# Masks of two batch pairs in one matmul, and instruction lists ordered by a new table, in a five-layer attention kernel

## The reference, cut to what matters

```python
def attention(q_src, kv_src, Wq, Wk, Wv, mask):      # in every layer
    scores = einsum("bhqd,bhkd->bhqk", heads(q_src @ Wq), heads(kv_src @ Wk)) / sqrt(8)
    return einsum("bhqk,bhkd->bhqd", softmax(where(mask, scores, -inf)), heads(kv_src @ Wv))

x = ln(x + attention(x, x, ...) @ Wo)                 # sa: no mask
x = ln(x + attention(x, ctx, ...) @ Wo)               # ca: head h sees keys k with (k - h) % 4 == 0
x = ln(x + gelu(x @ W1) @ W2)                         # f
x = ln(x + concat(x, attention(x, ctx, ...) @ Wout) @ Wupd)   # l1: one key mask per batch
x = ln(x + attention(x, ctx, ...))                    # l2: causal mask
x = x + gelu(x @ W1) @ W2                             # g
w = square(relu(scores(rmsnorm(x), rmsnorm(ctx))))    # l3: where |key - idx[token]| <= 1
x = x + (w / max(sum(w), 1e-6)) @ v @ Wo
```

## Time and profile before

| | |
|---|---|
| median of 3 runs | 227.08 us (224.49 to 230.85) |
| profiled execution | 224.79 us, span of its instructions 222.2 us |
| TensorE busy | 193.2 us, 4951 matmuls and as many weight loads |
| VectorE, ScalarE, GpSimd busy | 128.7, 119.9, 36.0 us |
| mean granted TensorE clock | 0.977 of full |

### The profile page before, as it was taken

One profiled execution on the slowest core, in us unless ns is written; L12 is line 12 of the kernel. 1 busy time (PEld: TensorE's weight loads), 2 busy tenths in 40 slices (PEclk: granted clock), 3 DMA queues, 4 the chain that ended last, 5 costly groups with the idle time before them and its releaser, 6 DMA issues.

```text
span 222.2 us, 11019 instructions
## 1 busy us (share of the span) xinstructions
PE 193.2 (87%) x4951; PEld 147.3 (66%) x4951; DVE 128.7 (58%) x227; ACT 119.9 (54%) x308; POOL 36.0 (16%) x61
## 2 busy tenths in 40 slices
PE   2798789999999999989798878899997799899935
PEld 0376568767886787668565656667686648588834
DVE  0599999996745227942378744442835226555950
ACT  1254740674756777477625652744769436763802
POOL 2990300131120131112011000111010003100000
PEclk9999996999999999999999999999999769999999
DMA  5990000000000000000000000000000000000002
GB/s 140 372 379 20 0 6 4 6 4 3 6 3 3 0 3 0 3 3 3 4 6 3 3 6 3 3 6 3 3 3 3 6 3 1 3 3 3 6 27 71
DMA packets 3901, 6.25 MB, mean 28 GB/s; under 512 B 528, under 2 KB 3216, under 8 KB 3600
## 3 DMA queue, kind: packets, MB, share of 16 engines
q1 hardware_dynamic: 3856, 5.57, 7.4%
HBM read 5.04 MB, written 0.52 MB: 25 GB/s over the span
## 4 chain that ended last, share of the span: by engine, by line
PE 67%; issue 9%; ACT 6%; DVE 5%; POOLq 1%; POOL 1%; DVEq 0%; ACTq 0%
PE bank L453 31%; PE score L456 20%; PE bank L697 12%; PE bank L669 4%; ACT probs_sb L801 2%; DVE probs_sb L1042 2%; ACT att_sb L845 1%; DVE m_col_sb L963 1%; POOLq L323 1%; DVE v_ext_sb L936 1%; DVE att_sb L1027 1%; ACT L801 1%; DVE v_ext_sb L933 1%; ACT xa_sb L850 0%; ACT probs_sb L799 0%
## 5 line engine op out<-in xcount | busy, mean ns | idle before, releaser
L963 DVE TENSOR_REDUCE m_col_sb<-score 128x32 f32<-128x2048 f32 (+1 forms) x16 | 30.2, 1889 | 11.8 <-PE score L456 11.6
L453 PE MATMUL bank<-v_ext_sb,probs_sb 128*32 128x18 f32 (+1 forms) x2176 | 28.5, 193 | 8.1 <-issue 6.4
L453 PEld LDWEIGHTS bank<-v_ext_sb,probs_sb 128*32 128x32 f32 x2176 | 24.7, 115 | 15.3 <-issue 13.5
L801 ACT ACTIVATE probs_sb<-score 128x1024 f32<-128x1024 f32 (+1 forms) x28 | 26.2, 962 | 13.0 <-PE score L456 12.9
L1082 POOL TENSOR_SCALAR vare_sb<-var_sb 128x2 f32<-128x2 f32 x20 | 5.2, 261 | 140.7 <-ACT att_sb L845 140.7
L453 PE MATMUL bank<-xa_sb,W_sb 128*128 128x256 f32 x64 | 21.3, 448 | 6.9 <-DMA W_sb<-in_mats 3.3
L905 DVE TENSOR_TENSOR k_heads_sb<-k_kept_sb,small_sb 128x1024 f32<-128x1024 f32 x12 | 14.7, 1226 | 16.5 <-ACT k_kept_sb L820 16.4
L914 DVE TENSOR_TENSOR q_heads_sb<-q_kept_sb,small_sb 128x1024 f32<-128x1024 f32 x16 | 19.5, 1222 | 6.5 <-ACT q_kept_sb L810 3.8
L845 ACT ACTIVATE att_sb<-bank 128x128 f32<-128x128 f32 x40 | 10.7, 274 | 21.5 <-PE bank L697 21.4
L456 PE MATMUL score<-k_heads_sb,q_kept_sb 32*64 32x256 f32 x384 | 18.0, 413 | 3.0 <-issue 2.2
L456 PE MATMUL score<-q_heads_sb,k_kept_sb 32*64 32x256 f32 x512 | 20.1, 400 | 0.4 <-issue 0.4
(11 more groups left out here) (120 smaller groups left out, 360.6 us busy)
## 6 DMA issues: line engine op xcount, KB each, us to landing
W_sb<-in_mats SPq DMA_DIRECT2D x1, 1152.0 KB, 7.6
W_sb<-in_mats SPq DMA_DIRECT2D x1, 1024.0 KB, 9.8
ctxT_sb<-in_ctxT SPq DMA_DIRECT2D x1, 512.0 KB, 5.1
cn_sb<-in_ctx SPq DMA_DIRECT2D x1, 512.0 KB, 11.3
hid_sb<-in_idx SPq DMA_DIRECT2D x1, 512.0 KB, 7.3
out<-attT_sb SPq DMA_DIRECT2D x4, 128.0 KB, 1.8
xa_sb<-in_xT SPq DMA_DIRECT2D x1, 384.0 KB, 3.9
W_sb<-in_mats SPq DMA_DIRECT2D x1, 192.0 KB, 2.8
```

The costliest lines, as they stand in the source:

```text
L453: return pe.matmul(o, l, r, start=start, stop=stop)
L801: act.activation(dst, src, ACT.Exp, scale=SCALE).then_inc(sem("exp"), 1)
L963: dve.tensor_reduce(o, src, AX.X, ALU.max).then_inc(sem("max"), 1)
```

## The change

1. Masks. In `scores` the loop over masks stands before the loop over j and a mask matmul writes both pairs at once: 512 columns, one x, one r. In `scores_t` the same for l2 and l3; l1's stays one j at a time, since its stationary operand is the key mask of the batch.
2. The planner. `records(k)` gives the number of instructions of each TensorE job, `fetched(...)` lets the program arrive in blocks of 256 of them, FETCH = 3.7 us apart, and delays a job by what has not arrived. Costs of pieces are replaced, SLOW is gone, HOP is 0.23 for 0.2, LEAD 8.3 for 5.3, and `AHEAD` is a new table, with entries for single groups as well ("flip_x ca 3").
3. Thereby the order of the lists of all engines.

```diff
+def records(k):
+
+    step, name, g, i = k
+    masks = {"s l1": 16, "s l2": 32, "t l1": 32, "t l2": 32, "t l3": 32}.get(f"{step} {name}", 0)
+    return masks + {"k": 5, "q": 5, "v": 9, "ctx_rows": 5, "m": 5, "flip": 5, "flip_x": 5, "h": 9, "y": 17, "ms": 9,
+                    "out": 17, "z": 44 if name == "f" else 20, "av": 66 if name == "ca" else 130, "s": 66,
+                    "t": {"ca": 83, "l3": 66}.get(name, 131), "weights": (21, 17, 5, 37, 11)[i % 5]}[step]
+
+
+def fetched(read, start, cost, n):
+
+    at, entered = read
+    end = start + cost
+    for block in range(at // BLOCK + 1, (at + n) // BLOCK + 1):
+        t = end - cost * (at + n - block * BLOCK) / n
+        end += max(0, entered + FETCH - t)
+        entered = max(t, entered + FETCH)
+    return end, (at + n, entered)
...
-        jobs[step, name, g, i] = (engine, cost * SLOW if engine == "pe" else cost, after)
+        jobs[step, name, g, i] = (engine, cost, after)
...
-                s = add("pe", {"ca": .5, "l2": 1.8, "l1": 1.5}.get(name, 1.2), "s", name, g, after=stacked)
+                s = add("pe", {"ca": .45, "l2": 1.6, "l1": 1.36}.get(name, 1.12), "s", name, g, after=stacked)
...
-            t = add("pe", {"ca": .5, "l1": 1.9, "l2": 2.1}.get(name, 1.7), "t", name, g, after=stacked)
+            t = add("pe", {"ca": .6, "l1": 1.62, "l2": 1.86, "l3": 1.48}.get(name, 1.42), "t", name, g, after=stacked)
...
-                k = [add("pe", .75, "av", name, g, i, after=[p, ("v_even", name, g)] + k
+                k = [add("pe", .62 if name == "ca" else .68, "av", name, g, i, after=[p, ("v_even", name, g)] + k
...
-            k = add("dve", .8, "divide", name, g, after=k)
+            k = add("dve", 1.03 if name == "l3" else .81, "divide", name, g, after=k)
...
-            k = add("pe", 2.2 if name == "f" else .95, "z", name, g,
+            k = add("pe", 2.64 if name == "f" else 1.3, "z", name, g,
...
-            urgency = way(k) - LEAD * g + AHEAD.get(step, 0) + AHEAD.get(f"{step} {name}", 0)
+            urgency = way(k) - LEAD * g + AHEAD.get(f"{step} {name}".strip(), 0) + AHEAD.get(f"{step} {name} {g}", 0)
...
+        if engine == "pe":
+            free[engine], read = fetched(read, start, cost, records(k))
...
-        end[k] = start + cost + (DMA_HOP if engine == "sp" else HOP)
+        end[k] = free[engine] + (DMA_HOP if engine == "sp" else HOP)
...
-HOP, DMA_HOP = 0.2, 2.0
-LEAD = 5.3
+HOP, DMA_HOP = 0.23, 2.0
+BLOCK, FETCH = 256, 3.7
+LEAD = 8.3
...
+AHEAD = {"attT ca": -18, "attT ca 1": 90, "attT ca 3": -72, "attT l2 1": -336, "attT l3 1": -270, "attT l3 2": -156,
+         "av l1": -39, "av l1 2": -54, "av l3": -63, "av l3 1": 93, "av sa 3": 84, "band": -396, "ctx_rows": -27,
+         "divide l3": -201, "divide l3 0": 21, "exp l1": 36, "exp l2": -51, "exp l2 2": -42, "exp l2 3": 123,
+         "exp sa": -111, "flip l1 1": -60, "flip l2": 30, "flip l2 1": -75, "flip l3 3": 60, "flip sa": 552,
+         "flip_x ca": -24, "flip_x ca 3": 147, "flip_x f": 36, "flip_x f 0": -33, "flip_x f 1": -6, "flip_x l1": 210,
+         "flip_x l1 3": -156, "flip_x sa": 141, "flip_x sa 2": -84, "flip_x sa 3": -96, "gelu f": -159, "gelu f 0": 54,
...
+                for n in range(masks):
+                    for x in range(2):
+                        for r in range(R):
+                            o = score[64 * x:64 * x + 64, r, :].rearrange("p (j h k) -> p j h k", j=NJ, h=HH)
+                            if name == "l1":
+                                row = km[rows_of(r, 1), tok(g)].rearrange("p (j x k) -> p j x k", j=NJ, x=2)[:, :, x, :]
+                                mm_onto(o, ones[rows_of(r, 1), 0:T], row.unsqueeze(2).to_broadcast([1, NJ, HH, T]),
+                                        start=True)
+                            else:
+                                mm_onto(o.rearrange("p j h k -> p (j h) k"), pattern("halves")[rows_of(r), n, :],
+                                        pattern("later")[rows_of(r), n, :].unsqueeze(1).to_broadcast([32, NJ * HH, T]),
+                                        start=n == 0)
                 for j in range(NJ):
-                    for n in range(masks + 1):
-                        for x in range(2):
-                            for r in range(R):
-                                o = score[64 * x:64 * x + 64, r, j * GT:j * GT + width]
-                                b = 2 * j + x
-                                if n == masks:
-                                    k = (kc_kept[rows_of(r), g, of_batch(b)] if name == "ca"
-                                         else k_heads[HEADS[name]][rows_of(r), g, :, of_batch(b)])
-                                    last = mm_onto(o, q_kept[rows_of(r), g, of_batch(b)], k, start=not masks)
-                                    continue
-                                oh = o.rearrange("p (h k) -> p h k", h=HH)
-                                if name == "l1":
-                                    t = (g * GB + b) * T
-                                    mm_onto(oh, ones[rows_of(r, 1), 0:T],
-                                            km[rows_of(r, 1), t:t + T].unsqueeze(1).to_broadcast([1, HH, T]), start=True)
-                                else:
-                                    mm_onto(oh, pattern("halves")[rows_of(r), n, :],
-                                            pattern("later")[rows_of(r), n, :].unsqueeze(1).to_broadcast([32, HH, T]),
-                                            start=n == 0)
+                    for x in range(2):
+                        for r in range(R):
+                            o = score[64 * x:64 * x + 64, r, j * GT:j * GT + width]
+                            b = 2 * j + x
+                            k = (kc_kept[rows_of(r), g, of_batch(b)] if name == "ca"
+                                 else k_heads[HEADS[name]][rows_of(r), g, :, of_batch(b)])
+                            last = mm_onto(o, q_kept[rows_of(r), g, of_batch(b)], k, start=not masks)
...
-                    for j in range(NJ):
+                    for j in range(NJ if name == "l1" else 1):
                         for x, r in tiles:
-                            t = (g * GB + 2 * j + x) * T
                             if name == "l1":
-                                stat = km[rows_of(r, 1), t:t + T]
-                                mov = ones[rows_of(r, 1), :].rearrange("p (h q) -> p h q", h=HH)
+                                t = (g * GB + 2 * j + x) * T
+                                mm_onto(place(x, r)[:, j, :, :], km[rows_of(r, 1), t:t + T],
+                                        ones[rows_of(r, 1), :].rearrange("p (h q) -> p h q", h=HH), start=j == 0)
+                                continue
+                            stat = pattern("halves")[rows_of(r), n, :]
+                            if name == "l2":
+                                mm_onto(place(x, r).rearrange("p j h q -> p (j h) q"), stat,
+                                        pattern("earlier")[rows_of(r), n, :].unsqueeze(1).to_broadcast([32, NJ * HH, T]),
+                                        start=n == 0)
                             else:
-                                stat = pattern("halves")[rows_of(r), n, :]
-                                mov = (pattern("earlier")[rows_of(r), n, :] if name == "l2"
-                                       else band[rows_of(r), n, t:t + T]).unsqueeze(1).to_broadcast([32, HH, T])
-                            mm_onto(place(x, r)[:, j, :, :], stat, mov, start=n == 0 and j == 0)
+                                mov = band[rows_of(r), n, tok(g)].rearrange("p (j x q) -> p j x q", j=NJ, x=2)[:, :, x, :]
+                                mm_onto(place(x, r), stat, mov.unsqueeze(2).to_broadcast([32, NJ, HH, T]), start=n == 0)
```

More of the change, by code:

```diff
@@ L94, in timetable @@
     w = [None] * 5
-    for i, (cost, kept, after) in enumerate(((2.6, .6, [load("w2")]), (2., .6, [load("w3")]), (.8, .3, []),
-                                             (3., .7, []), (.3, .5, []))):
+    for i, (cost, kept, after) in enumerate(((1.15, .68, [load("w2")]), (1.15, .68, [load("w3")]), (.5, .28, []),
+                                             (2.1, .77, []), (.35, .48, []))):
         before = {2: [w[0]], 3: [w[2]], 4: [w[3]]}.get(i, [])
@@ L114, in timetable @@
     for g in groups:
-        k = add("pe", .35, "ctx_rows", "", g, after=[ctx_scaled])
-        add("act", .3, "ctx_normed", "", g, after=[k])
+        k = add("pe", .28, "ctx_rows", "", g, after=[ctx_scaled])
+        add("act", .38, "ctx_normed", "", g, after=[k])
     for name in ATT:
@@ L142, in attention @@
         def attention(name, k):
-            k = add("pe", .6, "q", name, g, after=[k, load("w2" if name != "sa" else "w0")])
-            kept = [add("act", .42, "q_kept", name, g, after=[k, load("cols")])]
-            heads = [add("dve", 1.25, "q_heads", name, g, after=kept + [load("small")])] if name != "ca" else []
```

(17 more changed lines are left out.)

30 lines of the change are left out of this document (15 added, 15 removed), and 25 rows, old and new, of the table AHEAD.

## The result

| | before | after |
|---|---|---|
| median | 225.79 us (224.29 to 230.85, 4 runs) | 213.24 us (211.71 to 214.37, 4 runs) |
| profiled execution | 224.79 us, span 222.2 us | 214.37 us, span 212.5 us |
| mean granted clock in it | 0.977 | 0.984 |
| matmuls | 4951 | 4727 |
| issue waits of TensorE | 12.4 us in 15 | 8.8 us in 9 |

A forecast was written before the change was run, and what follows sets the result against it. TensorE was taken as the bound, stalling where its 256-record blocks arrive too slowly; 0.3 (masks) + 7.4 (order) + 1.3 (clock) - 1.0 (new waits) = 8.0 us less, 227.1 to 219.1 us, range 212.0 to 226.5.

The forecast's parts named there:

- rival (a): TensorE's list: the order pays in full, 10.5 of 12.4 us of issue waits and both clock falls go; 212 us, chance 0.17.
- the shift from profile to median: Whole run: the median of before, 227.08 us, lies 2.3 above its profiled execution, and the forecast is put on that scale.
- What bounds the kernel: TensorE: its program arrives in blocks of 256 records, one per 3.7 us at best, and denser stretches stall.
- The masks: Score and stacked pieces: merged masks save 0.3 us of columns; 448 fewer records save 2 to 3 us of stalls.
- The order: All engines' lists: block counting and better costs take 7.4 of 12.4 us of issue waits, merged records included; 5.0 stay.
- The clock: TensorE's half-clock falls near 36 and 176 us: the second goes in one case of two, worth 1.3 us.
- New waits: TensorE's in-order list, shared score buffer and late VectorE or ScalarE work: the new order costs 1.0 us.
- (b): TensorE: stalls turn into dependency waits of 15 us or more instead of 10; 226 us, chance 0.17.
- (c): TensorE: block arrival is hidden, issue waits go with the array or clock; 226.8 us, chance 0.03.
- (d): The end: group 3 trails, TensorE idle for over 10 of the last 20 us; 233 us, chance 0.07.
- signs named for the profile after: TensorE: 512-column masks at 0.43 to 0.46 us, 4727 matmuls, 37 or 38 packets, issue waits near 5 us mostly after 200.

The follow-up runs named there:

- spread fillers: The changed kernel with 53 or 64 small matmuls, over four column strips of the array, added behind the first k: 211.12 and 212.14 us.
- masks_only: The kernel before with the merged 512-column masks alone, planner and order as before: 218.80 us, the kernel before in the same rounds 229.68.
- spread_214: The changed kernel with 53 small matmuls (212 records) over four column strips behind the first k: 211.12 us, ratio to before 0.9238.
- searched: The changed kernel with its order improved by single-step search, block borders put 42 records earlier and mask pieces at their new lengths: 209.20 us.
- order_again: The changed kernel with the old 256-column masks, run again: 222.04 us against 228.67 of before, ratio 0.9732.
- spread_256: The changed kernel with 64 small matmuls (256 records, a whole block) over four column strips behind the first k: 212.14 us, ratio to before 0.9293.
- after_again: The changed kernel once more, unchanged, on the chip of the next comparisons: 213.51 us, ratio to before 0.9336.
- order_only: The changed kernel with the old loops over masks (256 columns): 220.68 us in three executions, a fourth at 416.71 left out.

## Why the prediction was right or wrong

The range (212.0 to 226.5) held 213.24 us, near its low end, and the side was right; the forecast of 219.1 us was 5.9 us too high. That the range held is in part luck: its low end was taken from rival (a), whose mechanism did not come, and the forecast's own range, 214.5 to 223.5, missed. Of the 5.9 us, 2.4 lie between the profiled executions (216.8 forecast, 214.37 measured), 2.3 are the shift from profile to median that I added, and 1.1 are the changed kernel's profiled execution over its own median.

**What bounds the kernel** held: blocks of 256 records, some 3.7 us apart. The two spread fillers show the 256, and so does the count of records ahead of every restart. The spacing is less constant than I wrote: 3.4 to 4.2 us between adjacent restarts in most places, 4.1 to 4.7 near the end in six kernels. "One per 3.7 us at best" was a misreading even of the trace I had: of the further pairs in it three are 3.7 to 3.9 us apart and not four, one is 4.20 and one 3.35 (175.81 to 179.16). The Trainium skill ("Runtime: NRT & Kernel Launch", section "Instruction fetch mechanics") has these blocks of 256 and calls their arrival hidden; here it was not, and the measurements decide.

**The masks** were the term most under-priced: 0.3 us of work, by the columns alone, and 2 to 3 us of records. The columns were right (0.46 us before and after); but the pieces lost 1.2 us in all, most of it the change from mask to data matmuls, which was there twice per score piece, and the records took 3.6 us off the issue waits. masks_only ended 5.6 us earlier between profiled executions and 8.9 and 10.9 us in the medians; in the new order the masks are worth 8.5. The whole piece stood in the timeline of before at 1.54 us, its masks at 0.24 + 0.21; I compared only the masks.

**The order.** I let 7.4 us of issue waits go, records included; 3.6 went in the profiled execution (5.7 with the ends of stalls that count as busy) and 8.8 stayed, over the 8 that I had named as the sign of an error. So this term was too high. One reason is one I did not look for: the planner's borders are 42 records off the real ones. The price of that is some 1 to 4 us (spread_214), more with a new search (searched). The order without the masks gained 6.6 us on its chip, in part through what is no issue wait: order_again still has 10.6 us of them.

**The clock.** 1.3 us forecast. The fall near 175 us, which I gave one chance in two, is gone, but a new one stands at 206.1 to 209.6 with TensorE busy throughout: of the recorded falls 1.9 us less busy time, 1.0 us. Another 1.4 us come from the start, where full clock came 2.7 us sooner, which I had no term for. So the recorded part is near the size forecast, though by other falls than I named. The shift to the median scale was a second error: I took 2.3 us from the profiled execution of before to its median and let the changed kernel keep it. It didn't: the changed kernel's profiled execution is the slowest of its first four. A part of before's surplus is its low clock (an execution at 0.953 had 21 us of half clock), and the changed kernel was at 0.968 or above in its eight runs; that fewer stalls are the reason is likely but not shown.

**New waits**: 1.0 us charged, none came; dependency waits are 9.3 us, before 9.8.

**Rivals.** (a)'s time, 212, was nearly met, but not by its mechanism: 10.5 us of issue waits did not go. (b) fails by its own sign, the dependency waits. (c) fails by the spread fillers. (d) fails: in the last 20 us TensorE is idle 20.0 - 13.5 = 6.5 us, not over 10. Of the signs named for the profile after, four came: 16 mask matmuls of 512 columns at 0.43 to 0.46 us, 4727 matmuls, 38 packets, and full clock near 175 us. Three did not: the busy time, 188.0, lies below the 190 to 193, the issue waits sum to 8.8 us and not to near 5, and 2.6 of them, not most, stand after 200 us.

## What to carry to other kernels

When a list of many small instructions stands still and waits for nothing, count its records between restarts: if they are multiples of one block apart, dense pieces need light ones between them, and a record taken away can be worth more than its own work (here 448 of them and 1.2 us of pieces took 5.6 us off the profiled execution). A planner that counts blocks must know where the first border lies; check it against one restart in a trace. Cost a merged instruction by the whole piece, from its first start to the next piece, not by its own columns, and compare the spread of runs before adding a shift between a profile and a median.

## What was not expected of the hardware

- 53 matmuls of 18 columns through one strip of the array took 5.8 us (55 ns per instruction of the trace); over four strips 1.7 us.
- The granted clock of one and the same program was 0.933 to 1.000 on average from run to run (the kernel before), with half-clock stretches behind some stalls of 1 to 2 us and none behind others. The average leaves out the start, where no clock is recorded and TensorE ran at half clock until 7.9 us in spread_256, 11.8 in after_again and 14.3 in the first profile of before.
- One execution of order_only took 416.71 us, with TensorE busy 98%; the same program took 220.3 to 223.2 us in seven others. Its score pieces of 32 matmuls of 256 columns took 2.56 to 2.60 us, where the same piece takes 2.01 at half clock and 1.12 at full clock, VectorE's busy time was as ever (129.9 us), and no issue wait is left. The trace has no record of the clock, and the 1.0 that its view gives says no more than that. Why it ran so stays unexplained.
- The time around the span was 2.6 to 3.0 us in the profiled executions of the kernel before and 1.8 to 1.9 in those of masks_only and of the changed one. That is left open, too.
